# A window-attention block: the output projection in column tiles, and its residual in four operations

## The chip, the cores and the metric

One core of one Trainium2 chip runs the kernel. The metric is the device time of one execution in microseconds (us), median of several runs.

## The reference

The input is x of 4 images, 96 channels, 128 x 128, in float32. Cut to what matters, with tokens as pixels:

```python
y = roll(layernorm(x, norm1), (-4, -4))            # then 8 x 8 windows: 64 tokens each
q, k, v = split(y @ qkv_w.T + qkv_b)               # 6 heads of 16 channels
attn = softmax(q @ k.T * 16 ** -0.5 + mask)        # in each window
out = (attn @ v) @ proj_w.T + proj_b               # 96 x 96: the projection
x2 = x + roll(out, (4, 4))                         # the first residual
h = gelu(layernorm(x2, norm2) @ mlp_w1.T + mlp_b1) # 384 hidden channels
x3 = x2 + (h @ mlp_w2.T + mlp_b2)                  # the second residual
result = x3 * rsqrt(gamma_eff @ x3 ** 2 + beta_eff)  # over the channels
```

## The kernel before, in words

The unit of work is a row of 16 windows; there are 64 of them, each worked on in two halves of 8 windows, which is 512 tokens (`HALF`). So each stage runs 128 times. Channels lie on the partitions and tokens along the free dimension, apart from the layer norms, for which TensorE transposes the tokens onto partitions (`turn_in`, called with 0 for the first norm and 1 for the second) and back (`turn_run`).

The kernel is written engine by engine. Each engine has a function `steps`, called once per round H, which issues one stage after another, each for a half of its own (H plus the stage's offset), so that halves overlap. The order on an engine is the order in `steps`; between engines there are semaphores, and an engine stops at a wait until it is fulfilled.

Around the change the order on TensorE is: `turn_run` (transposes of probabilities and normed tokens), `mlp_down` three times, `project`, `turn_in` 0 (of new image rows), `mlp_up` 0, `turn_in` 1 (of x2; it waits for `x2_ready`), `mlp_up` 1 and 2, and in the next round `scores`, `project_k`, `denominators`, `sum_probs`, `times_v`, `project_v`, `project_q`. On VectorE it is: `v_blocks`, `divide`, `outputs`, `split_y2`, `second_residual`, `first_residual`, `statistics` 0, `statistics` 1 (for which `turn_in` 1 must be done), and in the next round the maxima and shifts of the scores, and `normalise`. On ScalarE, `gelu` 0 to 2 wait for `mlp_up` 0 to 2; behind them come a table load and `k_copy`, for which `sum_probs` waits, since the bank of k is the one it uses next.

Six products share two PSUM banks (`mm_banks`) in turn; `mm_bank(name, A)` is the bank of an item, and `mm_wait` waits until its former content has been read. The projection's bank comes free with `x2_ready` and is then taken by `mlp_up` 1.

`divide`, `times_v` and `sum_probs` already use four column tiles. Of the 8 windows of a half, the first 6 (`MAIN` = 384 tokens) of head pairs 0 to 2 are at partitions 0 to 95 of `pv_bank`, and the last 2 (128 tokens) of all three head pairs are side by side at partitions 96 to 127. `divide` puts them together in `attended`: channels at partitions 0 to 95, row 96 all ones (for the bias), 512 tokens. Its last operation is line 833, its three small ones are line 831. `sum_probs` (lines 1091 and 1094) does three matmuls of 384 columns into partitions 0 to 95 and three of 128 columns into partitions 96 to 127.

A matmul of plain float32 is two passes, each a matmul of its own in the profile: 256 records for the 128 of `project` (line 1105). Those of line 999 (`in_parts`) are of rounded floats in three parts. `first_residual` is line 838, `second_residual` line 846, `outputs` line 853.

Of the kernel before, what the change touches and what calls it, by code (L numbers as in the profile page):

```python
# [22 lines left out]
N_IMAGES, DIM, HEIGHT, WIDTH = 4, 96, 128, 128  # L23
# [9 lines left out]
HALF = UNIT // 2  # L33
HALVES = 2 * UNITS
HALF_WINDOWS = WINDOWS // 2
PAIRS = HALF_WINDOWS // 2
HEAD_PAIRS = HEADS // 2
# [6 lines left out]
LAST = PAIRS - 1  # L44
MAIN = LAST * 2 * TOKENS
# [9 lines left out]
X_SLOTS = 4  # L55
# [7 lines left out]
def window_block(nc, x, qmask, kmask, ident, head_mask, ones_pair, norm1_w, norm1_b, qkv_t, qkv_b,  # L63
# [3 lines left out]
    ALU = mybir.AluOpType  # L67
# [4 lines left out]
    with ctx:  # L72
        def sb(name, shape, dt=f32):
            return ctx.enter_context(nc.sbuf_tensor(name, shape, dt))
# [4 lines left out]
        def sem(name):  # L79
            return ctx.enter_context(nc.semaphore(name))  # L80
# [12 lines left out]
        wproj = sb("wproj", [DIM + 1, DIM])  # L93
# [15 lines left out]
        x_ext = sb("x_ext", [DIM, X_SLOTS, WIN, WIDTH + SHIFT])  # L109
# [23 lines left out]
        attended = sb("attended", [DIM + 1, HALF])  # L133
        x2 = sb("x2", [DIM, 2, UNIT])
# [66 lines left out]
        proj_made = sem("proj_made")  # L201
        x2_ready = sem("x2_ready")
# [65 lines left out]
        def mm_bank(name, A):  # L268
            return mm_banks[MM_PLACE[name, A] % len(mm_banks)]
# [28 lines left out]
        def windows_of(tile, a):  # L298

            first = SHIFT + (a % 2) * (WIDTH // 2)  # L300
            return tile[:, :, first:first + WIDTH // 2].rearrange("c r (n w) -> c n r w", w=WIN)

        def in_windows(flat):
            return flat.rearrange("c (n r w) -> c n r w", r=WIN, w=WIN)
# [10 lines left out]
        def half_of(tile, a):  # L315
            return tile[:, (a % 2) * HALF:(a % 2 + 1) * HALF]

        def unit_slot(a, slots=2):
            return (a // 2) % slots
# [359 lines left out]
        def _(dve):  # L679
# [155 lines left out]

            def first_residual(A, a):
                dve.wait_ge(proj_made, A + 1)
                nc.vector.tensor_tensor(in_windows(half_of(x2[:, unit_slot(a), :], a)),
                                        in_windows(mm_bank("proj", A)[0:DIM, :]),
                                        windows_of(x_ext[:, unit_slot(a, X_SLOTS), :, :], a), ALU.add)\  # L840
                    .then_inc(x2_ready, 1)

            def second_residual(A, a):
                dve.wait_ge(mlp2_made, A + 1)
# [12 lines left out]
            def steps(run, H):  # L857

                run(max_scores, ATTEND, 0)
                run(max_scores, ATTEND, 1)  # L860
                run(shift_scores, ATTEND, 0)
                run(max_scores, ATTEND, 2)
                run(shift_scores, ATTEND, 1)
                run(shift_scores, ATTEND, 2)
                run(normalise, TURN_OUT, 0)
                run(normalise, MLP, 1)
                run(v_blocks, ATTEND)
                run(divide, PROJECT)
                run(outputs, DIVIDE)
                run(split_y2, MLP)  # L870
                run(second_residual, SETTLE)
                run(first_residual, PROJECT)
                run(statistics, TURN_IN, 0)
                run(statistics, PROJECT, 1)
                if H == -TURN_IN:
                    fold_qkv()
                if H == -TURN_IN + 1:
                    fold_mlp()
                if H == -TURN_IN + 2:
                    split_mlp()  # L880
# [3 lines left out]
            late(divide, FINAL)  # L884
            late(split_y2, FINAL - 1)
            late(first_residual, FINAL)
            late(second_residual, FINAL - 2)
            late(statistics, FINAL, 1)
# [13 lines left out]
        def _(pe):  # L902
# [14 lines left out]
            def mm_wait(name, A):  # L917
                found = mm_bank_emptied(name, A)
                if found is not None:
                    wait(pe, *found)  # L920
# [178 lines left out]
            def project(A, a):  # L1099
                if A == 0:  # L1100
                    pe.wait_ge(mlp_weights_ready, MLP_WEIGHTS)
                    pe.wait_ge(rows_set, 6)
                pe.wait_ge(attended_ready, A + 1)
                mm_wait("proj", A)
                nc.tensor.matmul(mm_bank("proj", A)[0:DIM, :], wproj[:, :], attended[:, :],  # L1105
                                 start=True, stop=True).then_inc(proj_made, 1)

            def mlp_up(A, a, n):
                if n == 0:
# [41 lines left out]
            def steps(run, H):  # L1151

                run(scores, ATTEND)
                run(project_k, QK)
                run(denominators, DIVIDE)
                run(sum_probs, ATTEND - 1)
                run(times_v, ATTEND - 1)
                run(project_v, ATTEND)
                run(project_q, QK)
                turn_run(H)  # L1160
                for n in range(HID_CHUNKS):
                    run(mlp_down, SETTLE, n)
                run(project, PROJECT)
                run(turn_in, TURN_IN, 0)
                if H == -TURN_IN:
                    qkv_bias_product()
                if H == -TURN_IN + 1:
                    w1_bias_product()
                run(mlp_up, MLP, 0)
                run(turn_in, PROJECT, 1)  # L1170
                run(mlp_up, MLP, 1)
                run(mlp_up, MLP, 2)
# [4 lines left out]
            turn_run(FINAL - 1 - MLP)  # L1177
            late(denominators, FINAL - 3)
            late(project, FINAL)
            for n in range(HID_CHUNKS):  # L1180
                late(mlp_down, FINAL - 2, n)
# [64 lines left out]
```

## Time and profile before

| | |
|---|---|
| median of 3 runs | 1769.26 us (1768.22 to 1774.46) |
| span of the profiled execution | 1766.9 us |
| TensorE busy (PE) | 1720.2 us, 97% |
| weight loads (PEld) | 1252.8 us, 71% |
| VectorE busy (DVE) | 1629.6 us, 92% |
| ScalarE busy (ACT) | 1527.5 us, 86% |
| GpSimd busy (POOL) | 1356.5 us, 77% |
| granted clock of TensorE, mean | 0.993 |

The span goes from the first to the last instruction of one profiled execution; the page gives no other time for that execution. Busy is time in which an engine has an instruction in work. The end of a matmul in the profile is modelled, and matmuls overlap: the time from start to start says more than a duration. "L838" is line 838 of the kernel. A line of a timeline merges like instructions that follow each other (x4: four of them, with the time from the first start to the last end), and has in brackets how long the engine sat idle before and what released it.

### The profile page before, as it was taken

To read this page: it belongs to the slowest core of one execution; us is meant where nothing else is said; L and a number is where in the kernel's file an instruction comes from. 1 tells how busy PE (TensorE), PEld (TensorE's weight loads), DVE (VectorE), ACT (ScalarE), POOL (GpSimd) and SP (SyncE) were. 2 spreads that over 40 slices of the span, in tenths; PEclk is the share of its full clock that TensorE was granted. 3 is DMA by queue.
4 is the path that set the end of the run, shared out by engine and by line. 5 is a ranking of instruction groups with operands and counts; after the bars stand their busy time and mean duration, and the time that the engine had idled before them with its cause. 6 is when DMAs were issued, how large, how long until landed. Compare 5 with 4: busy or idle time off the path is not lost.

```text
span 1766.9 us, 81406 instructions
## 1 busy us (share of the span) xinstructions
PE 1720.2 (97%) x32612; PEld 1252.8 (71%) x32612; DVE 1629.6 (92%) x4508; ACT 1527.5 (86%) x2832; POOL 1356.5 (77%) x1532
## 2 busy tenths in 40 slices
PE   4999999999999999999999999999999999999996
PEld 2677777777777777777777777777777777777763
DVE  5899999999999999999999999999999999999983
ACT  2798998988898988988898888998888898998986
POOL 3478878878878878878778877888878878878862
PEclk9999999999999999999999999999999999999997
DMA  2122122122122122122122122122122122122111
GB/s 58 27 46 52 37 54 52 37 54 53 37 53 52 36 54 52 38 53 52 36 55 52 36 55 50 37 56 52 35 56 49 37 56 51 37 55 52 28 32 27
DMA packets 215154, 81.35 MB, mean 46 GB/s; under 512 B 116118, under 2 KB 214780, under 8 KB 214780
## 3 DMA queue, kind: packets, MB, share of 16 engines
q1 hardware_dynamic: 214218, 76.04, 19.7%
q8 instruction: 261, 4.28, 1.0%
q14 instruction: 113, 0.93, 0.2%
q10 hardware_dynamic: 562, 0.11, 0.0%
HBM read 25.75 MB, written 25.17 MB: 29 GB/s over the span
## 4 chain that ended last, share of the span: by engine, by line
PE 96%; DVE 1%; issue 1%; ACT 1%; DMA 0%; SPq 0%; POOL 0%; POOLq 0%; DVEq 0%
PE mm_bank L999 49%; PE score_banks L1058 8%; PE score_banks L947 7%; PE mm_bank L1105 6%; PE mm_bank L1032 5%; PE pv_bank L1081 5%; PE turn_banks L939 5%; PE turn_banks L953 3%; PE mm_bank L1094 3%; PE mm_bank L1091 3%; PE score_banks L1066 1%; PE mm_bank L1134 0%; DMA x_ext<-in_x 0%; DVE stats L767 0%; SPq L378 0%
## 5 line engine op out<-in xcount | busy, mean ns | idle before, releaser
L457 POOL TENSOR_TENSOR hidden_lo<-hidden,hidden_hi 128x512 fp32r<-128x512 f32 x378 | 480.9, 1286 | 0.0
L618 ACT ACTIVATE hidden<-mm_bank 128x512 f32<-128x512 f32 x381 | 227.8, 598 | 124.1 <-PE mm_bank L999 111.8
L539 ACT ACT_TABLE_LOAD x253 | 324.6, 1283 | 4.5
L452 POOL TENSOR_SCALAR y_hi<-y 96x512 fp32r<-96x512 f32 x128 | 108.1, 845 | 206.8 <-ACT y L563 206.8
L812 DVE TENSOR_REDUCE row_max<-score_banks 128x8 f32<-128x512 f32 x384 | 250.8, 681 | 10.8 <-PE score_banks L1066 8.1
L820 DVE TENSOR_TENSOR shifted<-score_banks,row_max 128x512 f32<-128x512 f32 x384 | 250.7, 680 | 0.0
L469 POOL TENSOR_TENSOR x_sq<-x 96x512 f32<-96x512 f32 x126 | 130.8, 1038 | 152.2 <-DVE x L846 152.2
L585 ACT ACTIVATE probs<-shifted 128x512 f32<-128x512 f32 x384 | 236.2, 627 | 10.6 <-DVE shifted L820 3.4
L452 POOL TENSOR_SCALAR hidden_hi<-hidden 128x512 fp32r<-128x512 f32 x378 | 229.8, 619 | 1.3 <-ACT hidden L618 1.3
L597 ACT ACTIVATE probs_t<-score_banks 128x512 f32<-128x512 f32 x384 | 215.1, 602 | 0.0
L767 DVE BATCH_NORM_STATS2 stats<-turn_banks 128x6 f32<-128x96 f32 x1024 | 191.1, 248 | 17.1 <-PE turn_banks L939 17.1
L947 PEld LDWEIGHTS score_banks<-ident_sb,probs 64*128 64x128 f32 x3072 | 148.3, 139 | 53.9 <-ACT probs L585 28.2
L947 PE MATMUL score_banks<-ident_sb,probs 64*128 64x64 f32 x3072 | 184.3, 230 | 1.6 <-issue 1.1
L999 PE MATMUL mm_bank<-y_hi,w_hi 97*128 97x512 f32 x381 | 172.1, 452 | 1.0 <-ACT hidden L618 0.6
L457 POOL TENSOR_TENSOR y_lo<-y,y_hi 96x512 fp32r<-96x512 f32 x128 | 164.3, 1284 | 1.1 <-POOL y_hi L452 1.1
L457 POOL TENSOR_TENSOR x_sq_lo<-x_sq,x_sq_hi 96x512 fp32r<-96x512 f32 x126 | 160.9, 1277 | 0.7 <-POOL x_sq_hi L452 0.7
L999 PE MATMUL mm_bank<-hidden_hi,w_hi 128*96 128x512 f32 x378 | 160.6, 425 | 0.0
L776 DVE TENSOR_TENSOR turn_banks<-turn_banks,moments 128x384 f32<-128x384 f32 x256 | 145.0, 567 | 8.8
L1058 PE MATMUL score_banks<-k_block,q 32*64 32x128 f32 x6144 | 148.6, 275 | 3.9 <-DMA k_block<-k 2.5
L999 PE MATMUL mm_bank<-y_lo,w_hi 97*128 97x512 f32 x381 | 151.4, 397 | 0.0
L999 PE MATMUL mm_bank<-y_hi,w_lo 97*128 97x512 f32 x381 | 150.5, 395 | 0.0
L999 PE MATMUL mm_bank<-hidden_hi,w_lo 128*96 128x512 f32 x378 | 149.7, 396 | 0.0
(132 smaller groups left out, 4489.2 us busy)
## 6 DMA issues: line engine op xcount, KB each, us to landing
x_ext<-in_x SPq DMA_DIRECT2D x128, 192.0 KB, 2.9
k_block<-k SPq DMA_DIRECT2D x768, 32.0 KB
out<-o_ext SPq DMA_DIRECT2D x128, 192.0 KB, 2.6
w_raw<-in_w_t SPq DMA_DIRECT2D x1, 144.0 KB
w<-in_w_t SPq DMA_DIRECT2D x1, 144.0 KB
qkv_raw<-in_qkv_t ACTq DMA_DIRECT2D x1, 108.0 KB
ident_sb<-in_ident SPq DMA_DIRECT2D x1, 64.0 KB, 2.2
q_quadrants<-in_qmask SPq DMA_DIRECT2D x3, 1.0 KB
```

The source lines that it names most:

```text
L452: nc.gpsimd.tensor_scalar(hi, whole, 1.0, 1.0, ALU.mult, ALU.mult).then_inc(hi_ready, 1)
L457: nc.gpsimd.tensor_tensor(lo, whole, hi, ALU.subtract).then_inc(is_split, 1)
L539: nc.scalar.preload_act_table_set(name)
L585: nc.scalar.activation(probs[:, g, :, :, :].rearrange("t p j k -> t (p j k)"), shifted[:, g, :, :].rearrange("t i k -> t (i k)"), ACT.Exp)\
L597: nc.scalar.activation(dst, src, ACT.Copy).then_inc(probs_t_ready, 1)
L618: nc.scalar.activation(hidden_of(A)[:, n, :], up_bank(A, n), ACT.Gelu).then_inc(gelu_ready, 1)
L767: made = nc.vector.bn_stats(stats[ln][:, c, :], turn_banks[:, ln, n * DIM:(n + 1) * DIM])
L812: nc.vector.tensor_reduce(row_max[:, g, :], group_scores(g), op=ALU.max, axis=AX.X)\
L820: nc.vector.tensor_tensor(shifted[:, g, :, :], group_scores(g), row_max[:, g, :].unsqueeze(2) .broadcast_to([128, PAIRS * TILE_HEADS, TOKE ...
L947: return nc.tensor.transpose(score_banks[:, bank, first:first + TOKENS], probs[half, m, p, :, :], ident_sb[half, half])
L999: made = nc.tensor.matmul(out, w, x_part, start=first and part == 0, stop=last and part == 2)
L1058: made = nc.tensor.matmul(score_banks[64 * n:64 * n + 64, r, cols], q[rows, unit_slot(a), (w + n) * TOKENS:(w + n + 1) * TOKENS], k_block[ ...
```

## The change

The projection's one matmul of 96 rows of output and 512 columns becomes six: three of 32 output channels each for the first 384 tokens, into partitions 0 to 95 as before, and three for the last 128 tokens, all into partitions 96 to 127, side by side. The first residual, which adds the image, follows: three operations on 32 partitions x 128 tokens, which read PSUM at partition 96 and the image at partitions 0, 32 and 64 and write x2 there, and one on 96 x 384. `x2_ready` is signalled by the last.

```diff
             def first_residual(A, a):
                 dve.wait_ge(proj_made, A + 1)
-                nc.vector.tensor_tensor(in_windows(half_of(x2[:, unit_slot(a), :], a)),
-                                        in_windows(mm_bank("proj", A)[0:DIM, :]),
-                                        windows_of(x_ext[:, unit_slot(a, X_SLOTS), :, :], a), ALU.add)\
-                    .then_inc(x2_ready, 1)
+                to, image = half_of(x2[:, unit_slot(a), :], a), windows_of(x_ext[:, unit_slot(a, X_SLOTS), :, :], a)
+                for g in range(HEAD_PAIRS):
+                    rows = slice(32 * g, 32 * g + 32)
+                    nc.vector.tensor_tensor(in_windows(to[rows, MAIN:HALF]),
+                                            in_windows(mm_bank("proj", A)[DIM:128, g * 128:(g + 1) * 128]),
+                                            image[rows, 2 * LAST:HALF_WINDOWS, :, :], ALU.add)
+                nc.vector.tensor_tensor(in_windows(to[:, 0:MAIN]), in_windows(mm_bank("proj", A)[0:DIM, 0:MAIN]),
+                                        image[:, 0:2 * LAST, :, :], ALU.add).then_inc(x2_ready, 1)
...
                 mm_wait("proj", A)
-                nc.tensor.matmul(mm_bank("proj", A)[0:DIM, :], wproj[:, :], attended[:, :],
-                                 start=True, stop=True).then_inc(proj_made, 1)
+                for g in range(HEAD_PAIRS):
+                    rows = slice(32 * g, 32 * g + 32)
+                    nc.tensor.matmul(mm_bank("proj", A)[rows, 0:MAIN], wproj[:, rows], attended[:, 0:MAIN],
+                                     start=True, stop=True)
+                for g in range(HEAD_PAIRS):
+                    rows = slice(32 * g, 32 * g + 32)
+                    made = nc.tensor.matmul(mm_bank("proj", A)[DIM:128, g * 128:(g + 1) * 128], wproj[:, rows],
+                                            attended[:, MAIN:HALF], start=True, stop=True)
+                made.then_inc(proj_made, 1)
```

## Rows read from the trace of the kernel before

**Rows 1.** The page: busy time of each engine, and the chain that ended last, by engine.

```profile
PE 1720.2 (97%) x32612; PEld 1252.8 (71%) x32612; DVE 1629.6 (92%) x4508; ACT 1527.5 (86%) x2832; POOL 1356.5 (77%) x1532
...
PE 96%; DVE 1%; issue 1%; ACT 1%; DMA 0%; SPq 0%; POOL 0%; POOLq 0%; DVEq 0%
```

**Rows 2.** Windows (us; busy PE, PEld, DVE, ACT, POOL; PEclk): two periods, then `divide` to `divide`.

```profile
898.32:911.38 13.06, 13.06 (x251) 9.51 (x249) 12.60 (x36) 11.87 (x23) 10.52 (x11) 1.00 0.11 18
911.38:924.68 13.30, 13.30 (x258) 9.83 (x255) 12.78 (x37) 11.88 (x23) 11.07 (x14) 1.00 0.32 78
911.19:924.27 13.08, 13.08 (x257) 9.61 (x253) 12.57 (x36) 11.81 (x23) 10.97 (x14) 1.00 0.33 78
```

**Rows 3.** Line 833, the last operation of `divide`: duration min/median/max, first and last start.

```profile
L833 DVE TENSOR_TENSOR attended<-pv_bank,inv_sum x128: 553/554/556, 52.9 to 1734.3; 96x384 f32<-96x384 f32 x128
```

**Rows 4.** Timeline of all engines around the change: start us, us, engine, line.

```profile
913.31 0.39 PE L999 MATMUL mm_bank<-hidden_lo,w_hi 128*96 128x512 f32 x1
...
913.54 1.02 PE L1105 MATMUL mm_bank<-attended,wproj 97*96 97x512 f32 x2
...
913.79 0.74 DVE L846 SCALAR_TENSOR_TENSOR x<-mm_bank,b_col,x 96x512 f32<-96x512 f32 x1
...
914.41 0.49 PE L939 MATMUL turn_banks<-ident_sb,x_ext 96*128 96x96 f32 x4
...
914.61 0.69 DVE L838 TENSOR_TENSOR x<-mm_bank,x_ext 96x512 f32<-96x512 f32 x1
...
915.21 0.74 DVE L767 BATCH_NORM_STATS2 stats<-turn_banks 128x6 f32<-128x96 f32 x4
915.23 0.40 PE L999 MATMUL mm_bank<-y_lo,w_hi 97*128 97x512 f32 x1
915.35 0.43 PEld L939 LDWEIGHTS turn_banks<-ident_sb,x 96*128 96x128 f32 x4 [0.15 <-DVE x L838]
...
915.46 0.50 PE L939 MATMUL turn_banks<-ident_sb,x 96*128 96x96 f32 x4
...
916.30 0.40 PE L999 MATMUL mm_bank<-y_lo,w_hi 97*128 97x512 f32 x1
...
916.73 1.28 ACT L618 ACTIVATE hidden<-mm_bank 128x512 f32<-128x512 f32 x2
...
918.03 1.28 ACT L539 ACT_TABLE_LOAD   x1
...
920.21 0.52 PE L1091 MATMUL mm_bank<-probs_t,ones_pair_sb 128*32 128x384 f32 x3
```

**Rows 5.** Waits: who waited for whom, us in total, times, longest us.

```profile
PEld turn_banks L939 <- DVE x L838: 13.6, 84, 0.6
```

**Rows 6.** Timelines of TensorE: into the row sums and out of them, and `project_v` to `project_q`.

```profile
908.28 0.88 PE L1032 MATMUL mm_bank<-wv,y 97*32 97x48 f32 x64
909.09 0.47 PE L999 MATMUL mm_bank<-y_hi,wq_hi 97*96 97x512 f32 x1
...
1715.11 0.39 PE L999 MATMUL mm_bank<-x_sq_lo,wgdn_hi 97*96 97x512 f32 x1
1715.43 0.52 PE L1091 MATMUL mm_bank<-probs_t,ones_pair_sb 128*32 128x384 f32 x3
...
1715.80 0.49 PE L1094 MATMUL mm_bank<-probs_t,ones_pair_sb 128*32 128x128 f32 x3
1716.10 0.30 PE L1081 MATMUL pv_bank<-probs_t,v_block 128*32 128x64 f32 x8
```

**Rows 7.** Timeline of VectorE from `v_blocks` through `divide` to `outputs`.

```profile
923.29 0.95 DVE L803 TENSOR_TENSOR v_block<-mm_bank,ones_pair_sb 128x768 f32<-128x768 f32 x1
924.27 0.91 DVE L831 TENSOR_TENSOR attended<-pv_bank,inv_sum 32x128 f32<-32x128 f32 x3
925.19 0.55 DVE L833 TENSOR_TENSOR attended<-pv_bank,inv_sum 96x384 f32<-96x384 f32 x1
925.67 0.68 DVE L853 TENSOR_TENSOR o_ext<-x,inv_den 96x512 f32<-96x512 f32 x1
```


## The prediction

> **What bounds the kernel now.** I read the page's busy shares and its chain first: TensorE is busy 97% of the span and 96% of the chain that ended last is TensorE, so the kernel looks like one bound by matmuls, with VectorE second at 92% [rows 1]. Both shares are averages over 128 halves that all look alike, so the next view is two successive periods, cut at the start of the MLP's down projection (`mlp_down`), 898.32 to 911.38 to 924.68: 13.06 and 13.30 us, TensorE busy in all of either, VectorE 12.60 and 12.78 us, ScalarE 11.9, GpSimd 10.5 to 11.1, TensorE's granted clock 1.00 [rows 2]. The second is the half with the mask matmuls of the last window. From the first to the last `divide` there are 1734.3 - 52.9 = 1681.4 us, that is 127 periods of 13.24 us [rows 3].
>
> "Busy" does not say who is late for whom. That is in the timeline of all engines around the change [rows 4], and the reader should follow one signal in it, `x2_ready`. The projection starts at 913.54; `second_residual` runs on VectorE from 913.79 to 914.53; `first_residual` starts at 914.61, when the projection's result is there, and ends at 915.30. Meanwhile TensorE does `turn_in` of the next image rows (914.41) and `mlp_up` 0, whose last matmul starts at 915.23. The weight load of the second `turn_in`, which needs x2, starts at 915.35, 0.05 us after the residual's end, and its matmuls at 915.46. The last matmul in front takes 0.23 us from start to start, as 913.31 to 913.54 shows, so TensorE would have got there at 915.46 anyway. So the path through x2 has no slack and costs nothing either: it is exactly as long as the work that covers it. The waits say the same for the whole run: this load waited for L838 84 times, 13.6 us in all, mean 0.16 [rows 5].
>
> Behind this point TensorE's queue is in order (`mlp_up` 1 and 2, scores, keys, denominators, sums), and ScalarE hangs on it too: `mlp_up` 1 is made at 916.30 + 0.40 = 916.70, its gelu starts at 916.73, then come the table load at 918.03 and the key copy behind it, for which the row sums at 920.21 wait [rows 4]. A late x2 therefore moves both TensorE's and ScalarE's work by the same amount; I find nothing behind it that would take the lateness up.
>
> **The projection's matmuls.** Out goes one matmul of 97 x 512, two passes: from 913.54 to the next start at 914.41, 0.87 us [rows 4]. In come three of 384 columns and three of 128, in tiles of 32 columns. The kernel has exactly this set already, in `sum_probs`: start to next start 1715.43 to 1716.10, 0.67 us, the last result at 1715.80 + 0.49, so 0.86 us after the start [rows 6]. The six pay for changing the tile shape on either side. In: behind a full-width matmul the tiled ones start 0.32 us later (1715.11 to 1715.43), where full-width ones follow each other in 0.23: 0.09 more. Out: behind the tiled v projection the next full-width matmul starts 0.81 us after the group (908.28 to 909.09) though the group ends at 909.16; bounded below by 0 and above by one switch of the other kind, I take 0.1 [rows 6]. The sum is 0.09 + 0.67 + 0.1 = 0.86 against 0.87: TensorE gains nothing, with 0.2 us per half as the other end if the switches were free. The result is ready at 913.31 + 0.32 + 0.86 = 914.49 instead of about 914.56.
>
> The Trainium skill, TensorEngine Tiling (Array Packing), Key Properties, says that changing the tiling mode drains TensorE. The rows show the next group starting at 0.32 us where the matmul in front is recorded for 0.39 [rows 6]: by the rule in full, the result would be 0.07 us later, at 914.56, hence the first small residual 0.04 us later than below, 5 us over the run. I stay with the rows.
>
> **The first residual.** Out goes one operation of 96 x 512: 0.69 us, and 0.60 us of VectorE's time (914.61 to 915.21) [rows 4]. In come three of 32 x 128 and one of 96 x 384, the shapes of `divide`, which also reads partitions 96 to 127 of PSUM and writes 0, 32 and 64. There the three take 924.27 to 925.19 = 0.92 us, the large one 0.55 us to its end and 0.48 to the next start [rows 7]. So 0.92 + 0.55 = 1.47 us until `x2_ready` and 1.40 us of VectorE's time. The bounds: if small ones overlapped as the large ones do, 512 columns hand over after 0.60 us and 384 after 0.48, so 128 would after 0.48 - 2 x 0.12 = 0.24, and the four take 3 x 0.24 + 0.55 = 1.27 until the signal; upward, a mixed read of PSUM at 96 and x_ext at 0 to 64 has no row, and I allow 0.1 more for each small one, 1.77. I take 1.47, since the rows of `divide` have the same shapes and partition moves.
>
> The Trainium skill, VectorE: DVE Perf Modes, section on two Vector instructions with no wait between them, gives a rule for this: an operation whose input or output starts in another group of 32 partitions than the last one in that memory starts only when all before it are done. The trace agrees: 0.92 us for three of 0.29 to 0.30, no overlap, while the large one hands over 0.07 us early [rows 7]. By the rule all four would be held here too and `x2_ready` would come 1.47 us after the start, as in the sum by rows; by it rival 1 would be out.
>
> The start: `second_residual` stands in front in VectorE's queue and ends at 914.53, and v_block to `divide` shows 0.03 us from an end to a small operation [rows 4, 7]. So the first small one starts at 914.55, not at 914.49: an earlier projection is worth at most 0.06 us, whatever TensorE saves. `x2_ready` then comes at 914.55 + 1.47 = 916.02 instead of 915.30, which is 0.72 us later. TensorE's waiting load starts at 916.07, its matmuls at 916.18; work that stood in the cover ends where it did, so TensorE idles some 0.7 us there.
>
> **VectorE as a whole.** From one `divide` to the next, 911.19 to 924.27, are 13.08 us, 12.57 of them busy; most of the rest are short waits of statistics on themselves [rows 2]. Air is only in front of `first_residual`: `second_residual` could hand over at 914.45, 0.08 us before its end as others do, and the next starts at 914.61 [rows 4]. So VectorE needs 13.08 - 0.16 = 12.9 us. It gets 1.40 - 0.60 = 0.80, and 0.1 because a small operation does not overlap the one in front, as v_block shows [rows 7]: 13.8. The path through x2 gives 13.06 + 0.72 = 13.78 and 13.30 + 0.72 = 14.02 in turn. So the path decides, but VectorE is level with it in every other half.
>
> **Sum.** 127 periods x 0.72 = 91 us. The profiled span is 1766.9, so 1858. The page has no time of the profiled execution beside its span; the runs' median is 2.4 us above the span (launch and end), so 1861.
>
> **Beside other work, at no cost:** the projection's six extra weight loads run under its own matmuls, as in `sum_probs`; GpSimd's work starts from `second_residual`, which does not move, and gets 0.7 us more room; ScalarE's first gelu comes from the cover and is not later. No DMA changes; `load_x` waits for `x2_ready` four units back.
>
> **Rivals.**
> 1. *Small operations overlap.* They start when the projection is done, about 914.51, and x2 is ready at 914.51 + 1.27 = 915.78, 0.48 late: 127 x 0.48 = 61 us, 1830. For it: large ones do overlap. Against it: `divide`. 0.12.
> 2. *VectorE becomes the bound and the two lines add up.* VectorE at 13.8 is level with the path; if its waits no longer fall together, or small ones cost 0.1 more each, a half costs 0.2 to 0.3 more: 127 x 0.95 = 121 us, 1890. For it: VectorE has 0.16 us of air. Against it: its other waits move with the same path. 0.13.
> 3. *Not slower: the cover holds.* TensorE has `turn_in` and `mlp_up` 0 to do between the projection and x2, up to 915.46. If the four operations end by 915.35, 0.80 us after 914.55, nothing is late, and TensorE keeps what the tiles save: 0 to 0.2 us x 127, 1744 to 1769. It decides at three small ones in 0.25 us, 0.08 each, below anything of VectorE's that moves 128 columns in the rows. 0.04, of which 0.02 is faster.
> 4. *TensorE's saving is real.* Switches free, 0.2 us less: the work moves up in front of a wait that is bound by VectorE, so it changes the forecast by nothing; only the idle time grows. It is no case of its own.
>
> The forecast has 0.69, its own range 1845 to 1875. The last 0.02 is for more than rival 2. About 0.5%, 9 us, is what can be told from no change; every case but the third is far above. The range 1825 to 1890 takes in rivals 1 and 2 at their centres. Faster 0.02, same 0.03, slower 0.95.
>
> **What would show it.** Four residual operations per half: 384 of 32 x 128 at about 294 ns and 128 of 96 x 384 at about 554, together 0.92 + 0.48 us of queue time. TensorE's load of the x2 transposes waits for L838's successor about 0.7 us in nearly every half, some 80 to 90 us in all, against 13.6. The projection's group takes 0.67 us. TensorE's busy share falls below 95%, VectorE's stays at 91 to 95%; the period is 13.8 and 14.0 in turn. Wrong if the small operations start before the one in front has ended, if that wait is under 0.4 us, or if gelu 1 no longer starts as soon as `mlp_up` 1 is done.

## The result and the profile after

The changed kernel takes 1866.13 us (median of 4 runs, 1863.25 to 1869.7) against 1769.2: ratio 1.0542, 95% interval 1.0520 to 1.0564. By the ratio it is slower by 96 us, where 92 were forecast (1861). The profiled execution's span is 1861.5 us, 94.6 more than before.

From the page of the changed kernel, busy times and the chain by engine, which answer to [rows 1]:

```profile
PE 1760.5 (95%) x33892; PEld 1281.0 (69%) x33892; DVE 1724.9 (93%) x4892; ACT 1540.1 (83%) x2832; POOL 1359.1 (73%) x1532
...
PE 61%; DVE 29%; issue 8%; ACT 1%; DMA 0%; SPq 0%; DVEq 0%; POOL 0%; POOLq 0%
```

VectorE is busy for 95 us more. The chain, 96% TensorE before, now goes through VectorE for 29% of the span.

Line 833 of the changed kernel, first and last `divide` (answers to [rows 3]): (1829.3 - 53.4) / 127 = 13.98 us per period, 0.74 more than 13.24.

```profile
L833 DVE TENSOR_TENSOR attended<-pv_bank,inv_sum x128: 552/553/556, 53.4 to 1829.3; 96x384 f32<-96x384 f32 x128
```

The timeline around the change (answers to [rows 4]; columns: start, us, engine, line). Lines 1111 and 1115 are the new projection, 841 and 844 the new residual, 943 the transposes:

```profile
920.25 0.40 PE L1003 MATMUL mm_bank<-hidden_lo,w_hi 128*96 128x512 f32 x1
...
920.58 0.52 PE L1111 MATMUL mm_bank<-attended,wproj 97*32 97x384 f32 x3
...
920.95 0.49 PE L1115 MATMUL mm_bank<-attended,wproj 97*32 97x128 f32 x3
...
921.37 0.55 PE L943 MATMUL turn_banks<-ident_sb,x_ext 96*128 96x96 f32 x4
921.53 0.91 DVE L841 TENSOR_TENSOR x<-mm_bank,x_ext 32x128 f32<-32x128 f32 x3
...
922.25 0.40 PE L1003 MATMUL mm_bank<-y_lo,w_hi 97*128 97x512 f32 x1
922.45 0.55 DVE L844 TENSOR_TENSOR x<-mm_bank,x_ext 96x384 f32<-96x384 f32 x1
...
923.06 0.37 PEld L943 LDWEIGHTS turn_banks<-ident_sb,x 96*128 96x128 f32 x4 [0.85 <-DVE x L844]
923.06 0.56 PE L943 MATMUL turn_banks<-ident_sb,x 96*128 96x96 f32 x4 [0.42 <-DVE x L844]
...
923.40 0.48 PE L1003 MATMUL mm_bank<-y_hi,w_hi 97*128 97x512 f32 x1
...
924.37 1.30 ACT L618 ACTIVATE hidden<-mm_bank 128x512 f32<-128x512 f32 x2 [0.54 <-PE mm_bank L1003]
```

Count from the last down projection (920.25; 913.31 before). x2 is ready at 2.75 us instead of 1.99, which is 0.76 later. The transposes of x2 start at 2.81 instead of 2.15, only 0.66 later: before the change they started 0.16 us after x2 was ready, behind the matmul in front of them, and now they start 0.06 after it. So there was 0.10 us of slack. The first matmul of `mlp_up` 1 (915.74 before) follows at 3.15 instead of 2.43, 0.72 later, because from the transposes to it are now 0.34 us instead of 0.28. In about nine of ten halves this stretch is 3.13 to 3.15 us long, where it was 2.43 or 2.44. The gelu behind it, which before started when ScalarE was free, now waits 0.54 us.

Waits of the changed kernel, total, times, longest (answers to [rows 5]); the first is the weight load, the second the matmul engine itself:

```profile
PEld turn_banks L943 <- DVE x L844: 109.5, 127, 1.3
...
PE turn_banks L943 <- DVE x L844: 54.4, 127, 1.1
```

### The profile page after: what moved, and what is told of

It reads as the page before. It is cut to its first block, busy times and chain, and to the rows that moved or that the text cites. A ratio compares the mean times of both kernels' runs of the same rounds, so it can differ in the third digit from the quotient of the medians.

```text
span 1861.5 us, 84350 instructions
## 1 busy us (share of the span) xinstructions
PE 1760.5 (95%) x33892; PEld 1281.0 (69%) x33892; DVE 1724.9 (93%) x4892; ACT 1540.1 (83%) x2832; POOL 1359.1 (73%) x1532
## 4 chain that ended last, share of the span: by engine, by line
PE 61%; DVE 29%; issue 8%; ACT 1%; DMA 0%; SPq 0%; DVEq 0%; POOL 0%; POOLq 0%
PE mm_bank L1003 30%; DVE x L841 6%; PE score_banks L1062 5%; PE score_banks L951 5%; DVE x L844 4%; PE mm_bank L1036 3%; PE pv_bank L1085 3%; DVE row_max L812 3%; DVE stats L767 3%; PE turn_banks L943 3%; PE mm_bank L1115 2%; PE turn_banks L957 2%; PE mm_bank L1098 2%; PE mm_bank L1095 2%; DVE attended L831 2%
## 5 line engine op out<-in xcount | busy, mean ns | idle before, releaser
L452 POOL TENSOR_SCALAR y_hi<-y 96x512 fp32r<-96x512 f32 x128 | 112.2, 877 | 297.8 <-ACT y L563 297.8
L1003 PE MATMUL mm_bank<-hidden_lo,w_hi 128*96 128x512 f32 x378 | 149.9, 397 | 0.0
```

The costliest lines, as they stand in the source:

```text
L452: nc.gpsimd.tensor_scalar(hi, whole, 1.0, 1.0, ALU.mult, ALU.mult).then_inc(hi_ready, 1)
L1003: made = nc.tensor.matmul(out, w, x_part, start=first and part == 0, stop=last and part == 2)
```

## The experiments

Each kernel was timed in three rounds beside the kernel before. Ratios are to it, with the 95% interval.

**1. Each half of the change by itself.** The projection alone is the new `project` with the old `first_residual`. The residual alone:

```diff
-                                            in_windows(mm_bank("proj", A)[DIM:128, g * 128:(g + 1) * 128]),
+                                            in_windows(mm_bank("proj", A)[rows, MAIN:HALF]),
...
-                    nc.tensor.matmul(mm_bank("proj", A)[rows, 0:MAIN], wproj[:, rows], attended[:, 0:MAIN],
-                                     start=True, stop=True)
...
+                nc.tensor.matmul(mm_bank("proj", A)[0:DIM, :], wproj[:, :], attended[:, :],
+                                 start=True, stop=True).then_inc(proj_made, 1)
```

> The six tiled matmuls alone; the residual stays one operation of 96 x 512 (so the last quarter of the tokens, which lies at partitions 96 to 127, is not what it adds: that part of the output is left wrong). Theory (TensorE gains nothing, the switches of tile shape pay it back): 1769 us within 5. Rival (the tiles save 0.2 us per half where TensorE is the bound): 1744 to 1755.

> The projection stays one matmul; the residual is three operations of 32 x 128 and one of 96 x 384, each reading the partitions it writes. Theory (the whole loss is the residual's four operations, 1.47 us until x2 is ready): within 6 us of the changed kernel, 1860 to 1868. Rival (reading partition 96 and writing 0 to 64 is what makes small ones dear): about 1830.

Measured: the projection alone 1783.82 us, ratio 1.0062 (1.0041 to 1.0083); the residual alone 1864.86, ratio 1.0525 (1.0501 to 1.0549). The residual alone makes the whole loss, as the theory said. The projection is not free, as its theory (1769 within 5) had it, but costs some 11 us by the ratio. The timeline of the kernel with the projection alone shows where:

```profile
924.79 0.40 PE L999 MATMUL mm_bank<-hidden_lo,w_hi 128*96 128x512 f32 x1
925.12 0.52 PE L1107 MATMUL mm_bank<-attended,wproj 97*32 97x384 f32 x3
...
925.91 0.36 PEld L939 LDWEIGHTS turn_banks<-ident_sb,x_ext 96*128 96x128 f32 x4 [0.20 <-issue]
925.92 0.55 PE L939 MATMUL turn_banks<-ident_sb,x_ext 96*128 96x96 f32 x4
...
926.25 0.48 PE L999 MATMUL mm_bank<-y_hi,w_hi 97*128 97x512 f32 x1
```

0.33 us into the tiles, 0.80 to the transposes (0.67 of it the stream, so 0.13 to get out), 0.33 to `mlp_up` 0, which before was 0.27 (914.41 to 914.68). From the last down projection to `mlp_up` 0 it is 1.46 us against 1.37: 0.09 x 127 = 11 us. The 0.06 behind the transposes goes with their weight loads: here the first one starts with the matmuls, where before it ran 0.43 us ahead of them (914.41):

```profile
913.98 0.14 PEld L939 LDWEIGHTS turn_banks<-ident_sb,x_ext 96*128 96x128 f32 x1 [0.27 <-issue]
```

The late transposes of x2 in the changed kernel show the same (load and matmul both at 923.06, 0.34 us to the next group). No run took this apart. In the changed kernel the projection's 0.09 us is invisible: there TensorE waits for x2 anyway, and the two parts together (1866) take no more than the residual alone (1865).

**2. The price of the tile shape.** Three tiles of 32 columns over all 512 tokens, results where they were:

```diff
+                for g in range(HEAD_PAIRS):
+                    rows = slice(32 * g, 32 * g + 32)
+                    made = nc.tensor.matmul(mm_bank("proj", A)[rows, :], wproj[:, rows], attended[:, :],
+                                            start=True, stop=True)
+                made.then_inc(proj_made, 1)
```

> The projection as three tiled matmuls of 32 columns of weights by 512 tokens, results where they were, the residual one operation. The stream is as long as before (0.86 us) and both switches of tile shape are added (0.2 us). Theory: projection ready 0.09 us later and the next matmuls 0.2 us later, 127 x 0.1 to 0.2 = 13 to 25 us, 1782 to 1794. Rival (switches cost nothing here): 1769.

Measured: 1808.08 us, ratio 1.0196 (1.0170 to 1.0222), more than the theory's upper end.

```profile
922.87 0.40 PE L999 MATMUL mm_bank<-hidden_lo,w_hi 128*96 128x512 f32 x1
923.20 1.06 PE L1107 MATMUL mm_bank<-attended,wproj 97*32 97x512 f32 x6
924.18 0.55 PE L939 MATMUL turn_banks<-ident_sb,x_ext 96*128 96x96 f32 x4
924.52 0.48 PE L999 MATMUL mm_bank<-y_hi,w_hi 97*128 97x512 f32 x1
```

Here the same stretch is 1.65 us, 0.28 more than before: both switches cost 0.28 us together, not the 0.2 taken, and all of it goes into the time (127 x 0.28 = 36 us, 35 by the ratio). The fourth tile does save 1.65 - 1.46 = 0.19 us of it.

**3. Why small operations cost what they cost.** As the residual alone, but from the fifth half on all three small ones start at partition 0 everywhere, with the second and third result put aside:

```diff
+                    rows = slice(32 * g, 32 * g + 32) if A < 4 else slice(0, 32)
+                    small = to[rows, MAIN:HALF] if A < 4 or g == 0 else aside[:, g - 1, :]
```

> As the kernel with the residual alone in four operations, but from the fifth half on all three small ones read PSUM, image and write at partition 0 (the second and third into a buffer aside: two thirds of the last quarter of x2 are left as they were). Same number, shapes and order; only the start partitions differ. Theory (a small one waits for the one in front only where an operand changes its group of partitions): 3 x 0.24 + 0.55 = 1.27 until the signal, 0.5 us late, 1830. Rival (small operations never overlap): as with the partitions changing, 1862.

Measured: 1823.49 us, ratio 1.0299 (1.0271 to 1.0326). VectorE's timeline of this kernel:

```profile
915.15 0.74 DVE L852 SCALAR_TENSOR_TENSOR x<-mm_bank,b_col,x 96x512 f32<-96x512 f32 x1
915.92 0.28 DVE L843 TENSOR_TENSOR x<-mm_bank,x_ext 32x128 f32<-32x128 f32 x1
916.12 0.47 DVE L843 TENSOR_TENSOR aside<-mm_bank,x_ext 32x128 f32<-32x128 f32 x2
916.52 0.54 DVE L846 TENSOR_TENSOR x<-mm_bank,x_ext 96x384 f32<-96x384 f32 x1
```

And that of its pair, the residual alone:

```profile
937.42 0.74 DVE L850 SCALAR_TENSOR_TENSOR x<-mm_bank,b_col,x 96x512 f32<-96x512 f32 x1
...
938.19 0.88 DVE L841 TENSOR_TENSOR x<-mm_bank,x_ext 32x128 f32<-32x128 f32 x3
...
939.08 0.55 DVE L844 TENSOR_TENSOR x<-mm_bank,x_ext 96x384 f32<-96x384 f32 x1
```

The same shapes now start every 0.20 us, before the one in front has ended, and the four end 1.14 us after the first start instead of 1.44. So it is the change of the partition group, not the number of operations alone, that makes each small one cost its full duration. The Trainium skill, VectorE: DVE Perf Modes, section on two Vector instructions with no wait between them, states this rule; the pair of runs agrees, 0.30 us per small operation where an operand changes its group (0.31 in the changed kernel) and 0.20 where none does.

Two operations, 96 x 128 and 96 x 384, both from partition 0:

```diff
+                nc.vector.tensor_tensor(in_windows(to[:, MAIN:HALF]), in_windows(mm_bank("proj", A)[0:DIM, MAIN:HALF]),
+                                        image[:, 2 * LAST:HALF_WINDOWS, :, :], ALU.add)
```

> The projection stays one matmul; the residual is two operations, 96 x 128 and 96 x 384, both from partition 0. Theory (no overlap only where an operand changes its group of 32 partitions; no slack before x2): x2 ready 0.24 + 0.55 = 0.79 instead of 0.69 after the start, 127 x 0.10 = 13 us, 1782. Rival (every further operation costs its whole 0.3 us): 0.17 late, 1790. Rival (there is slack of 0.1 us): 1770.

Measured: 1776.49 us, ratio 1.0032 (1.0015 to 1.0049): 6 us, between the theory's 13 and the 1 of the rival with 0.1 us of slack. In the trace:

```profile
915.36 0.39 PE L1000 MATMUL mm_bank<-hidden_lo,w_hi 128*96 128x512 f32 x1
...
916.65 0.29 DVE L839 TENSOR_TENSOR x<-mm_bank,x_ext 96x128 f32<-96x128 f32 x1
...
916.86 0.54 DVE L841 TENSOR_TENSOR x<-mm_bank,x_ext 96x384 f32<-96x384 f32 x1
...
917.55 0.50 PE L940 MATMUL turn_banks<-ident_sb,x 96*128 96x96 f32 x4
```

x2 is ready 2.04 us after the last down projection, only 0.05 later than before (the theory had 0.10), and the transposes start 0.15 after it, not the 0.06 that they show where x2 holds them up. So lateness of this size goes into the slack; where the 6 us come from stays open. Each run's loss fits a slack of 0.1: x2 0.05 late costs 0.3%, 0.45 late (the four that overlap) 3.0%, 0.76 late 5.3 to 5.4%.

**4. Is it x2's lateness or VectorE's work?** Both grew by about 0.75 us. First, VectorE's work is cut away from x2's path, in the changed kernel and in the one before:

```diff
-                blocks = HALF_WINDOWS * HEAD_PAIRS
+                blocks = HALF_WINDOWS * HEAD_PAIRS if A < 2 else 4
```

> The changed kernel, but from the third half on v_blocks fills 4 of 24 blocks (the others keep old values), which takes 0.67 us per half off VectorE, away from the path through x2. Theory (the path through x2 is the bound, VectorE only level with it): 1860 to 1866, at most 6 us less. Rival (VectorE's whole work is the bound): 0.4 to 0.67 us less per half, 1781 to 1815.

> The kernel before with the same light v_blocks. Theory (TensorE and the path through x2 bound it, VectorE has 0.16 us of air): 1765 to 1769. Rival (VectorE is the bound before too): 1700 or less.

Measured: the changed kernel with light v_blocks 1868.21 us, ratio 1.0541 (1.0514 to 1.0568; the changed kernel has 1.0542); the one before with it 1768.04, ratio 0.9987 (0.9970 to 1.0004). VectorE is busy for 68 us less and nothing is gained in either. The time turned into waits for TensorE (waits of the changed kernel with light v_blocks):

```profile
PEld turn_banks L943 <- DVE x L844: 109.0, 127, 1.3
...
DVE x L850 <- PE mm_bank L1003: 49.0, 125, 1.7
```

x2's wait is the same 109 us as in the changed kernel. So the path through x2 is the bound, not VectorE's work as a whole.

Then the reverse, work added behind the signal, so that x2 is not late by it:

```diff
                 dve.wait_ge(x_turned[ln], A + 1)
+                if ln == 0:
+                    for g in range(HEAD_PAIRS):
+                        nc.vector.tensor_tensor(aside[32 * g:32 * g + 32, :], turn_banks[96:128, 0, 0:128],
+                                                ident_sb[96:128, :], ALU.add)
```

> The kernel before, with three further operations of 32 x 128 at the head of the first statistics, behind the residual's signal: each reads PSUM at partition 96 and a constant, and writes a buffer aside at 0, 32 and 64, as in divide; the result is unchanged. x2 is not late by them. VectorE needs 12.9 + 0.92 + 0.11 = 13.95 us per half. Theory (VectorE was nearly full, so such work makes it the bound wherever it stands): 127 x 0.7 = 90 us more, 1850 to 1865. Rival (only what stands before the signal counts): 1769 to 1775.

Measured: 1877.48 us, ratio 1.0594 (1.0572 to 1.0617), above the theory's range by 12 us. Timeline of VectorE and the projection in this kernel:

```profile
914.63 1.02 PE L1111 MATMUL mm_bank<-attended,wproj 97*96 97x512 f32 x2
...
914.92 0.74 DVE L852 SCALAR_TENSOR_TENSOR x<-mm_bank,b_col,x 96x512 f32<-96x512 f32 x1
...
915.69 0.69 DVE L844 TENSOR_TENSOR x<-mm_bank,x_ext 96x512 f32<-96x512 f32 x1
...
916.41 0.91 DVE L770 TENSOR_TENSOR aside<-turn_banks,ident_sb 32x128 f32<-32x128 f32 x3
...
917.33 0.76 DVE L773 BATCH_NORM_STATS2 stats<-turn_banks 128x6 f32<-128x96 f32 x4
```

From one `divide` to the next it is 14.07 us (912.32 to 926.39). VectorE has one wait left in it. The residual starts 0.77 us after `second_residual`, when the projection is made (914.63 + 1.02 = 915.65). Where the projection is long made, as in the kernel of experiment 5 with its operations behind `divide`, it starts 0.66 us after, while `second_residual` still runs:

```profile
903.37 1.02 PE L1110 MATMUL mm_bank<-attended,wproj 97*96 97x512 f32 x2
...
904.58 0.74 DVE L851 SCALAR_TENSOR_TENSOR x<-mm_bank,b_col,x 96x512 f32<-96x512 f32 x1
...
905.24 0.68 DVE L843 TENSOR_TENSOR x<-mm_bank,x_ext 96x512 f32<-96x512 f32 x1
```

So of the 14.07 us, 0.92 + 0.12 are the new work and 0.77 - 0.66 = 0.11 is the wait for the projection. The remaining 12.92 are what VectorE needed before, the forecast's 12.9. The wait is 127 x 0.11 = 14 us, about what the run lies above the range. By the waits TensorE is late too, through the softmax: ScalarE's exponentials waited for VectorE's shifts of the scores, and TensorE needs them before it comes to the projection; no run tested this by itself (waits of this kernel, then of the kernel before):

```profile
ACT probs L586 <- DVE shifted L826: 112.9, 242, 1.8
```

```profile
ACT probs L585 <- DVE shifted L820: 3.4, 8, 1.8
```

So x2's lateness is what counts in the changed kernel, but the rival (only what stands before the signal counts) is out: work behind it costs as much once VectorE is full. The changed residual makes VectorE's need 12.92 + 0.80 + 0.11 = 13.83 us; the 0.11 is there because its first operation does not overlap `second_residual` (in 48 halves of the changed kernel it starts 0.77 us after it, in none earlier).

**5. The same with inputs from SBUF.** A first version of this experiment read both inputs from SBUF, behind the residual, from `y_tok`; then with a constant as source (as in experiment 4, VectorE waits once, at the start, for the constant to be loaded), behind `divide` and behind the residual:

```diff
+                for g in range(HEAD_PAIRS):
+                    nc.vector.tensor_tensor(aside[32 * g:32 * g + 32, :], ident_sb[96:128, :],
+                                            ident_sb[96:128, :], ALU.add)
```

> The kernel before with three further operations of 32 x 128 behind the residual, after its signal, each with an operand in a new group of partitions, which add nothing to the result. x2 is not late by them; VectorE needs about 12.9 + 1.05 = 13.95 us per half instead of 13.28. Theory (VectorE was nearly full, any 0.8 us or more makes it the bound wherever it stands): 1845 to 1860. Rival (only what stands before the signal counts): 1769 to 1775.

> The kernel before, with three further operations of 32 x 128 behind divide that read both inputs from SBUF and write aside. In the earlier run such operations behind the residual took 497 ns on average (283 to 1004) instead of 294. Theory (they are slow only while GpSimd works, which is mostly idle behind divide): about 290 to 320 ns each, 1850 to 1865. Rival (two inputs from SBUF make them slow as such): about 500 ns, 1930 or more.

> The same three operations behind the residual instead, where GpSimd squares x3. Theory (slow while GpSimd works): about 500 ns each, as in the earlier run with another source, about 1980. Rival (the source of the earlier run, which was being read by TensorE's transposes in other halves, made it slow): about 290 ns, 1860.

Measured: 1982.63 us for the first (ratio 1.1190, 1.1149 to 1.1231), 1912.88 behind `divide` (1.0797, 1.0774 to 1.0821), 1978.74 behind the residual (1.1164, 1.1113 to 1.1215). The first missed theory and rival, the second lies between them, the third is what its theory said. Durations, min/median/max in ns, of these operations behind `divide`, behind the residual, and of those of experiment 4 that read PSUM:

```profile
L838 DVE TENSOR_TENSOR aside<-ident_sb x384: 282/285/706, 53.6 to 1880.2; 32x128 f32<-32x128 f32 x192
```

```profile
L845 DVE TENSOR_TENSOR aside<-ident_sb x384: 283/608/908, 56.6 to 1949.8; 32x128 f32<-32x128 f32 x192
```

```profile
L770 DVE TENSOR_TENSOR aside<-turn_banks,ident_sb x384: 291/293/298, 7.1 to 1776.2; 32x128 f32<-32x128 f32 x192
```

The same instruction takes 285 ns in one place and 608 in the other. Behind the residual GpSimd is at work; behind `divide` it mostly is not, and there the group gets slow where it is:

```profile
902.11 1.25 DVE L838 TENSOR_TENSOR aside<-ident_sb 32x128 f32<-32x128 f32 x3
902.60 0.62 POOL L453 TENSOR_SCALAR y_hi<-y 96x512 fp32r<-96x512 f32 x1 [1.26 <-ACT y L564]
```

Two of 0.285 end at 902.70; the third begins within GpSimd's operation and takes until 903.36. That is 0.14 us after GpSimd's operation has ended (902.60 + 0.62 = 903.22). The whole trace of this kernel shows the same: 121 of the 384 operations start while a GpSimd operation runs, and 118 of these take 605 to 706 ns; the 263 others take 282 to 288. Behind the residual 251 start within one, and 250 of them take over 500. So it is the GpSimd operation already running that holds them up, and the forecast of 290 to 320 ns missed because behind `divide` the second or third of them starts within one in most halves (the mean was 392 ns). The source of the first run was not the cause. I did not take GpSimd's work away, so this rests on the overlap in time. It bears on neither kernel of the change, whose small operations read PSUM and keep to 294 ns.

## Why the prediction was right

The mechanism was right: x2 comes late by VectorE's four operations, and TensorE and ScalarE wait for it. The last digits owe something to luck, as the first and third points say.

1. *The path through x2 has no slack.* Right in the main: periods alternate between 13.8 and 14.0 us (forecast 13.78 and 14.02), apart from some longer ones, and lighter work on VectorE gains nothing. But there were 0.10 us of slack. The forecast's 0.72 comes out at `mlp_up` 1 because three small misses cancel: x2 is 0.76 late (0.72 forecast), 0.10 of it goes into the slack, and the transposes take 0.06 longer to the next group. The forecast took the 0.11 us from the weight load (915.35) to its matmuls (915.46) as needed; where x2 is late, both start together (923.06).
2. *The first residual costs what `divide` costs.* Right to the row: 0.92 us for the three, 0.55 for the large one (922.45 to 923.00), means 294 and 554 ns. That the mixed partitions of PSUM and image might cost more did not come true. Rival 1 was the right question: without the change of partition group the run came to 1823, near its 1830 (x2 1.14 - 0.69 = 0.45 late, 0.48 in the rival). What the change does rules it out.
3. *TensorE gains nothing.* Nearly right. The stretch costs 0.09 us more rather than 0.01 less. The term that was too small is the way out of the tiles: 0.13 to the transposes and 0.06 behind them, where 0.1 was taken. It cost nothing here, because it lies before a wait. The first small operation starts 1.28 us after the last down projection (forecast 1.24); in the half shown it waited for the projection (0.85 after `second_residual`), not for `second_residual` as the forecast had it. This is not where the missing 4 us are: of the 0.74 us that a period grew, 0.72 lie between the last down projection and `mlp_up` 1, as forecast, and the residual alone, with the projection as before, takes 1865 as well. The 0.02 left, some 3 us in all, lie behind `mlp_up` 1; their cause is open.
4. *VectorE is level with the path.* Right, term by term: 12.92 + 0.80 + 0.11 = 13.83 against 13.8 (experiment 4). Rival 2, both adding up, did not happen: the period is the path's. But experiment 4 shows how near it stood: 1877 us with VectorE full, though x2 came as soon after the last down projection as before.
5. *What would show it.* The load's wait for x2 was put at 0.7 us and 80 to 90 us in all; it is 0.86 and 109.5, since it counts from the last weight load and was 0.15 before. TensorE's own idle time there is only 0.43 us, as the matmul in front is recorded beyond its successor's possible start: 922.25 + 0.23 = 922.48 to 923.06 are 0.58. TensorE's share is 1760.5 / 1861.5 = 94.6%, just below the 95% named. The gelu still starts 0.04 us after `mlp_up` 1 is made (923.94 + 0.39 = 924.33).

No version here beats the kernel before; the nearest is the two operations from partition 0, 0.3% slower.

## What to carry to other kernels

A result that is moved to a free tile has to be fetched from there: count VectorE's operations, and a full duration for each that starts in another group of 32 partitions, before counting what TensorE saves. Look in the timeline for the first matmul that waits for the result. How long after the result it starts, less what it takes when the result alone holds it up (0.16 - 0.06 = 0.10 us here), is all the slack there is; here, of what lay beyond it, nearly all went into the period. That its weight load waits does not yet mean that the matmul is late. A switch of tile shape and back costs 0.28 us here, so a tiled group that stands alone among full-width matmuls must save more than that.

## What was not expected of the hardware

A small VectorE operation with both inputs in SBUF took 285 ns alone and 608 in the median (up to 1004 in one run) where it started while a GpSimd operation ran, and it ended 0.14 us after that one. With one input in PSUM it took 291 to 298 ns wherever it stood. Four transposes whose first weight load could not run ahead of them took 0.33 to 0.34 us to the next group instead of 0.27 to 0.28.
